# Cross attention with layer norm on one core: two buffers for the doubled queries, a compact K spread by DMA, V placed by halves

## What is computed

```python
qs = (q @ wq).reshape(Bq, Lq, H, HD).transpose(0, 2, 1, 3)
ks_ = (k @ wk).reshape(Bq, Lk, H, HD).transpose(0, 2, 1, 3)
vs = (v @ wv).reshape(Bq, Lk, H, HD).transpose(0, 2, 1, 3)
scores = jnp.einsum('bhqd,bhkd->bhqk', qs, ks_) / jnp.sqrt(jnp.float32(HD))
scores = jnp.where(mask[:, None, :, :], -jnp.inf, scores)
attn_w = jax.nn.softmax(scores, axis=-1)
attn = jnp.einsum('bhqk,bhkd->bhqd', attn_w, vs)
attn = attn.transpose(0, 2, 1, 3).reshape(Bq, Lq, H * HD)
out = attn @ wo + q
mu = jnp.mean(out, axis=-1, keepdims=True)
var = jnp.mean((out - mu) ** 2, axis=-1, keepdims=True)
return (out - mu) / jnp.sqrt(var + EPS) * gamma + beta
```

## Time and profile before

| | us |
|---|---|
| median of 3 runs | 651.32 |
| lowest and highest | 650.71, 651.92 |
| the profiled execution, its own time | 653.43 |
| its span, first to last instruction | 651.6 |
| granted clock, mean over the span | 0.987 |
| PE busy in the span | 612.8 (94%) |
| DVE, ACT, POOL busy | 526.4, 507.1, 493.8 |

### The profile page before, as it was taken

One profiled execution on the slowest core, in us unless ns is written; L12 is line 12 of the kernel. 1 busy time (PEld: TensorE's weight loads), 2 busy tenths in 40 slices (PEclk: granted clock), 3 DMA queues, 4 the chain that ended last, 5 costly groups with the idle time before them and its releaser, 6 DMA issues.

```text
span 651.6 us, 12679 instructions
## 1 busy us (share of the span) xinstructions
PE 612.8 (94%) x3840; PEld 477.7 (73%) x3840; DVE 526.4 (81%) x1008; ACT 507.1 (78%) x1558; POOL 493.8 (76%) x639
## 2 busy tenths in 40 slices
PE   7999879989999999999999999999999999999895
PEld 5676667777868777787867777786877778687763
DVE  5887667778879888888879787887888888787887
ACT  4877867878878788887978888797977888786750
POOL 5476548787968879797986879698886979576784
PEclk9999998999999999999999999999999999998998
DMA  8853455282743628273552728255361826534103
GB/s 284 211 138 104 120 146 146 74 219 81 189 146 106 169 73 220 82 203 122 137 161 95 198 69 222 101 156 156 104 185 64 226 83 163 194 100 128 49 33 114
DMA packets 47794, 90.80 MB, mean 139 GB/s; under 512 B 10096, under 2 KB 13168, under 8 KB 47728
## 3 DMA queue, kind: packets, MB, share of 16 engines
q1 hardware_dynamic: 47728, 90.00, 48.5%
HBM read 39.53 MB, written 16.78 MB: 86 GB/s over the span
## 4 chain that ended last, share of the span: by engine, by line
PE 47%; DVE 15%; DMA 13%; ACT 9%; SPq 8%; issue 4%; POOL 4%; POOLq 0%; DVEq 0%; ACTq 0%
PE bank L486 14%; PE bank L391 13%; DMA qd<-qn 12%; ACT pr L604 6%; SPq L295 4%; PE bank L428 4%; PE bank L459 4%; PE bank L438 3%; DVE pr L745 3%; PE bank L413 3%; DVE nm L751 3%; DVE sm L758 2%; SPq L267 2%; PE bank L464 2%; DVE al L767 2%
## 5 line engine op out<-in xcount | busy, mean ns | idle before, releaser
L604 ACT ACTIVATE pr<-pr,nm 128x77 f32<-128x77 f32 x1024 | 269.8, 348 | 61.8 <-DVE nm L751 59.4
L916 POOL TENSOR_TENSOR pn<-pr,rec 128x512 f32<-128x512 f32 x128 | 134.8, 1053 | 102.1 <-DVE rec L760 97.0
L745 DVE SCALAR_TENSOR_TENSOR pr<-msk,bank 128x308 f32<-128x308 uint8 x256 | 109.4, 468 | 55.9 <-PE bank L428 50.4
L391 PE MATMUL bank<-xh,wqh 128*128 128x512 f32 x256 | 104.9, 410 | 3.1 <-DVE ql L733 2.3
L758 DVE TENSOR_REDUCE sm<-pr 128x8 f32<-128x616 f32 x128 | 99.8, 779 | 9.8 <-ACT pr L604 8.6
L486 PE MATMUL bank<-woh,ah 128*128 128x512 f32 x256 | 105.5, 412 | 1.5 <-DVE al L767 1.4
L751 DVE TENSOR_REDUCE nm<-pr 128x8 f32<-128x616 f32 x128 | 101.8, 795 | 4.4
L566 ACT ACTIVATE ptr<-bank 128x512 f32<-128x512 f32 (+1 forms) x256 | 95.5, 427 | 11.8 <-PE bank L438 11.6
L486 PE MATMUL bank<-wol,ah 128*128 128x512 f32 x256 | 102.6, 401 | 0.0
L486 PE MATMUL bank<-woh,al 128*128 128x512 f32 x256 | 102.4, 400 | 0.0
L391 PE MATMUL bank<-xh,wql 128*128 128x512 f32 x256 | 100.7, 393 | 0.0
(11 more groups left out here) (81 smaller groups left out, 999.0 us busy)
## 6 DMA issues: line engine op xcount, KB each, us to landing
qd<-qn SPq DMA_DIRECT2D x120, 256.0 KB, 4.6
xraw<-xT SPq DMA_DIRECT2D x58, 256.0 KB, 3.1
xres<-x SPq DMA_DIRECT2D x58, 256.0 KB, 2.8
out<-y SPq DMA_DIRECT2D x56, 256.0 KB, 2.1
ptr<-xT SPq DMA_DIRECT2D x6, 256.0 KB, 9.4
zt<-x SPq DMA_DIRECT2D x6, 256.0 KB, 4.3
out<-zt SPq DMA_DIRECT2D x6, 256.0 KB, 2.0
wk_sb<-wk SPq DMA_DIRECT2D x4, 256.0 KB, 4.4
```

The costliest lines, as they stand in the source:

```text
L391: last = nc.tensor.matmul(misc_bank(("q", i))[:], w[:, k, m * P:(m + 1) * P], s[:, blk % 2, k, :], start=(k == 0 and n == 0), stop=(k == K ...
L604: last = nc.scalar.activation(s, s, ACT.Exp, bias=nm[:, t % 2, h:h + 1], scale=1.0)
L745: nc.vector.scalar_tensor_tensor(out=pr[:, 4 * g:4 * g + 4, :], in0=msk[:, b % 2, t % TB, :].unsqueeze(1).broadcast_to([P, 4, LK]), scalar ...
L916: nc.gpsimd.tensor_tensor(pn[:, half, 0:4, :].rearrange("p s (e k) -> p (s e) k", e=2), pr[:, hs, 0:KM], rec[:, t % 2, hs].unsqueeze(2).br ...
```

## The change

**Doubled q.** `qd` gets a second buffer: block blk uses `qd[:, blk % 2]`. `double_q(i)` now copies one part (four DMAs of 64 rows by 512 values, half of the bytes each), with a semaphore `d_qd[m]` per part, as soon as ACT has kept that part; it waits for the scores of the block two before. The calls stand in tiles t % 4 = 1, 2, 3 (for part i = t + 3) and a second one in t % 4 = 3 (i = t + 4).

**K.** `keep_k` and `low_k` are one instruction each per group of heads (128 rows) and write compact tensors `khc` and `klc`. `spread` copies them with four DMAs of 32 rows on the diagonals of `kh`, which now holds one batch; `place_kh(b, i)` does this for groups 2i and 2i + 1 when the last tile of the batch before has read them (tiles 15, 31, 47). `kd` holds two batches and is filled by `place_kd(b)`, eight DMAs, in tiles 1, 12, 20 and 36. Before tile 0 PE waits for the spread high part (`d_kh[0]`) and low part (`d_kl`, kept in the second buffer of `kd`, which is called `kl`).

**Scores.** Block 0 has three matmuls of 308 columns per group; from tile 4 on all tiles use `qd` and `kd`. In each block's first tile PE waits for one part's copies at each group. `project_q(3)` now stands ahead of the first scores, not behind.

**V.** `place_v(b, e)` does half of the rows of a batch. Batch 0's halves are in tile 0, the other six in tiles 3 to 8, one in each; PE and ACT wait per batch (`d_vb`).

```diff
-DOUBLES = {2: 4, 4: 6}
+KD_AT = {1: 0, 12: 1, TB + 4: 2, 2 * TB + 4: 3}
-PLACE = {0: (0, 0), 2: (1, 1), 4: (2, 1), 5: (3, 2)}
+PLACE = {3: (1, 0), 4: (1, 1), 5: (2, 0), 6: (2, 1), 7: (3, 0), 8: (3, 1)}
...
-        kh = sb("kh", [P, NG, NB, GW], f32r)
-        kd = sb("kd", [P, NG, 2, NB, PW], f32r)
+        khc = sb("khc", [P, NG, NB, LK], f32r)
+        klc = sb("klc", [P, NG, NB, LK], f32r)
+        kh = sb("kh", [P, NG, GW], f32r)
+        kd = sb("kd", [P, 2, NG, 2, PW], f32r)
...
-        qd = sb("qd", [P, 2, NG, D], f32r)
+        qd = sb("qd", [P, 2, 2, NG, D], f32r)
...
+            def spread(dst, src, sig):
+
+                for j in range(4):
+                    rows = slice(32 * j, 32 * j + 32)
+                    sp.dma_start(dst[rows, :, j * LK:(j + 1) * LK].bitcast(f32), src[rows].bitcast(f32)).then_inc(sig, 16)
+
+            def place_kh(b, i):
+
+                sp.wait_ge(p_s, NG * (TB * b - 1) + 2 * i + 2)
+                spread(kh[:, 2 * i:2 * i + 2], khc[:, 2 * i:2 * i + 2, b], d_kh[i])
+
+            def place_kd(b):
+
+                if b >= 1:
+                    sp.wait_ge(p_s, NG * max(4, TB * (b - 1)))
+                for v, src in enumerate((khc, klc)):
+                    for j in range(4):
...
             def double_q(i):
 
                 blk, m = i // 4, i % 4
-                if blk > 1:
-                    sp.wait_ge(p_s, NG * (4 * blk - 1) + m + 2)
-                elif m > 0:
-                    sp.wait_ge(p_s, NG * (PLAIN + 1))
-                sp.wait_ge(a_qh, i + 2)
+                if blk >= 2:
+                    sp.wait_ge(p_s, NG * 4 * (blk - 1))
+                sp.wait_ge(a_qh, i + 1)
                 for u in range(2):
                     for v in range(2):
-                        sp.dma_start(qd[64 * v:64 * v + 64, u, m:m + 2].bitcast(f32), qn[64 * u:64 * u + 64, m:m + 2].bitcast(f32)
-                                     ).then_inc(d_qd[m // 2], 16)
+                        sp.dma_start(qd[64 * v:64 * v + 64, blk % 2, u, m].bitcast(f32), qn[64 * u:64 * u + 64, m].bitcast(f32)
+                                     ).then_inc(d_qd[m], 16)
...
-                if t % 4 == 3 and 3 < t < T - 4:
-                    double_q(t + 1)
+                if t in KD_AT:
+                    place_kd(KD_AT[t])
+                if 1 <= t <= T - 4 and t % 4 > 0:
                     double_q(t + 3)
+                if t % TB == TB - 1 and t < T - 1:
+                    place_kh(t // TB + 1, 0)
+                    place_kh(t // TB + 1, 1)
+                if t % 4 == 3 and t < T - 4:
+                    double_q(t + 4)
...
-                    if r == 0 or t == PLAIN + 1:
-                        pe.wait_ge(d_qd[g // 2], 64 * blk)
...
+                    if r == 0:
+                        pe.wait_ge(d_qd[g], 64 * blk)
+                    if t == 4 or t > 4 and t % TB == 0:
+                        pe.wait_ge(d_kd[t // TB % 2], 128 * (t // TB // 2 + 1))
...
             def keep_k(g):
                 act.wait_ge(p_k, g + 1)
-                for j in range(4):
-                    rows = slice(32 * j, 32 * j + 32)
-                    nc.scalar.activation(kh[rows, g, :, j * LK:(j + 1) * LK],
-                                         bank[g][rows, 0:NB * LK].rearrange("p (b k) -> p b k", b=NB), ACT.Copy,
-                                         scale=SCALE).then_inc(a_k, 1)
+                nc.scalar.activation(khc[:, g].rearrange("p b k -> p (b k)"), bank[g][:, 0:NB * LK], ACT.Copy,
+                                     scale=SCALE).then_inc(a_k, 1)
```

More of the change, by code:

```diff
@@ L166, in cross_attention_layernorm @@
         d_wv = sem("d_wv")
-        d_vm = [sem(f"d_vm{i}") for i in range(2)]
+        d_vb = [sem(f"d_vb{b}") for b in range(NB)]
         d_msk, d_gb = [sem(f"d_msk{i}") for i in range(2)], sem("d_gb")
@@ L172, in cross_attention_layernorm @@
         d_y = [sem(f"d_y{i}") for i in range(YS)]
-        d_kd = [sem(f"d_kd{g}") for g in range(NG)]
-        d_k0 = [sem(f"d_k0{i}") for i in range(2)]
-        d_qd = [sem(f"d_qd{i}") for i in range(2)]
+        d_kh = [sem(f"d_kh{i}") for i in range(2)]
+        d_kl, d_kd = sem("d_kl"), [sem(f"d_kd{i}") for i in range(2)]
+        d_qd = [sem(f"d_qd{g}") for g in range(NG)]
         d_end, d_xe = sem("d_end"), sem("d_xe")
@@ L280, in pair_k0 @@
-            def pair_k0(g):
-                sp.wait_ge(p_s, NG * PLAIN + g + 2)
-                sp.dma_start(kd[0:64, g:g + 2, 1, 0].bitcast(f32), kh[64:128, g:g + 2, 0, PW:GW].bitcast(f32)).then_inc(d_k0[g // 2], 16)
+                        for s in range(4):
+                            row = KM * e + KR * s + KR
+                            sp.dma_start(vr[row + KM - LK:row, b, :, s % 2, :],
+                                         vs[at + KM - lo:at + LK - lo, i, s, e]).then_inc(d_vb[b], 16)
@@ new lines, in spread @@
+            def spread(dst, src, sig):
[10 more added lines that the diff above has]
+                    for j in range(4):
+                        rows = slice(64 * v + 32 * (j % 2), 64 * v + 32 * (j % 2) + 32)
+                        sp.dma_start(kd[rows, b % 2, :, j // 2, j % 2 * LK:(j % 2 + 1) * LK].bitcast(f32),
+                                     src[32 * j:32 * j + 32, :, b].bitcast(f32)).then_inc(d_kd[b % 2], 16)
@@ L306, in _ @@
             sp.wait_ge(g_z, 1)
+            sp.wait_ge(a_k, NG)
+            spread(kh, khc[:, :, 0], d_kh[0])
+            sp.wait_ge(v_k, NG)
+            spread(kl, klc[:, :, 0], d_kl)
             for n in range(8, 10):
                 load_slice(n)
-            for g in range(NG):
-                pair_k(g)
             for k in range(2):
@@ L330, in _ @@
                     sp.wait_ge(g_vz, 1)
+                    sp.wait_ge(a_v, 1)
+                    place_v(0, 0)
+                    place_v(0, 1)
                 if t in PLACE:
-                    b, piece = PLACE[t]
-                    sp.wait_ge(a_v, piece + 1)
-                    place_v(b)
+                    b, e = PLACE[t]
+                    sp.wait_ge(a_v, (1, 2, 2, 3)[b])
+                    place_v(b, e)
                 if t in (TB + 1, 2 * TB + 1):
@@ L641, in _ @@
                 keep_x(k)
-            act.wait_ge(v_z, 1)
-            keep_k(0)
-            keep_k(1)
+            for g in range(NG):
+                keep_k(g)
             keep_q(0)
             keep_q(1)
-            keep_k(2)
             keep_x(4)
             keep_q(2)
-            keep_k(3)
             keep_x(5)
@@ L653, in _ @@
             keep_x(6)
+            keep_x(7)
             exps(0, 0)
-            keep_x(7)
             keep_v(0)
@@ L712, in low_k @@
             def low_k(g):
-                for j in range(4):
-                    rows = slice(32 * j, 32 * j + 32)
-                    dve.wait_ge(a_k, 4 * g + j + 1)
-                    nc.vector.scalar_tensor_tensor(
-                        out=(kd[rows, g, 1] if j >= 2 else kt[rows, g])[:, :, j % 2 * LK:(j % 2 + 1) * LK],
-                        in0=bank[g][rows, 0:NB * LK].rearrange("p (b k) -> p b k", b=NB), scalar=SCALE,
-                        in1=kh[rows, g, :, j * LK:(j + 1) * LK].bitcast(f32), op0=ALU.mult,
-                        op1=ALU.subtract).then_inc(v_k, 1)
+                dve.wait_ge(a_k, g + 1)
+                nc.vector.scalar_tensor_tensor(
+                    out=klc[:, g].rearrange("p b k -> p (b k)"), in0=bank[g][:, 0:NB * LK], scalar=SCALE,
+                    in1=khc[:, g].rearrange("p b k -> p (b k)").bitcast(f32), op0=ALU.mult, op1=ALU.subtract).then_inc(v_k, 1)
             def mask_all(b):
```

96 lines of the change are left out of this document (32 added, 64 removed).

## The result

| | before | changed |
|---|---|---|
| median of 4 runs, us | 651.37 | 629.62 |
| lowest and highest, us | 650.71, 651.92 | 629.06, 631.12 |
| profiled execution, us | 653.43 | 630.17 |
| its span, us | 651.6 | 628.4 |
| granted clock, mean | 0.987 | 0.998 |

The ratio is 0.967, with a 95% interval of 0.965 to 0.969. The forecast was 627.5 us, in a range of 621 to 642.

What follows compares the result with a forecast made beforehand. PE's own instruction list was taken as the bound. Gains and losses 18.3 - 2.0 + 6.4 + 1.5 - 1.2 + 0.8 = 23.8 us took the profiled 653.43 to 629.6, so 627.5 us for the median, range 621 to 642.

Steps and rivals of the forecast that it cites:

- rival D: Mid-kernel: another engine takes over once PE no longer pauses, half the stalls return as waits for ACT; 636 us, chance 0.07.
- Block turns, 18.3 us: Turns between blocks: PE's weight-load waits for copies into `qd` go with halved copies and a second buffer; gain 18.3 us.
- The landing, 3.7 us: Block turns: part 3's last copy lands 3.7 us after issue, taken between 2.7 and 4.6, so no stall.
- Rival B: Block turns: part 3's last copy still lands 5.6 us or more after issue, halving gains nothing; 642 us, chance 0.12.
- Batch turns, minus 2.0 us: Tiles 16, 32, 48: `kh`'s eight DMAs delay part 3's copies, 0.7 us late each; loss 2.0 us (1 to 10).
- V and x, 6.4 and 1.5 us: Tiles 1 to 8: x slices go out earlier; PE's gap and slow clock go (6.4), part of ACT's 3.00 wait (1.5).
- Tile 4, minus 1.2 us: Tile 4 now needs doubled q, part 3 kept only one tile earlier; PE waits 0 to 2.7 us, 1.2 taken.
- The first scores: Start: K's spread copies land at 25.1 us, PE comes at 25.7, no stall; at the other end 6.2 us lost.
- rival C: Start: low K lands behind x, costing 6.2 us and a slow clock of 2 to 3; 635 to 637 us, chance 0.12.
- Costed at nothing: Mid-kernel: `kd`'s DMAs in tiles 12, 20, 36 and SP's eight more issues per block, covered by SP's 266.0 us wait for POOL.
- Rival E: Whole kernel: SP becomes the bound, slower from 1.97 us an issue; 682 us at 2.1 us an issue, chance 0.04.
- Rival F: Block turns: stalls only move from `qd` to `kh` and the ring without a gain; 651 us, chance 0.03.

Runs made afterwards that it cites:

- joined copies: Changed kernel with two buffers kept, but two parts of q in one copy (256 KB) as in the kernel before: 659.79 us, ratio 1.011.
- three kernels with idle DMAs: Changed kernel with eight, three or six small unread copies issued ahead of part 3's copies at ten ordinary turns: 671.05, 628.24 and 647.45 us.
- part 3 ahead: Changed kernel with part 3's copies of q issued ahead of the second half of `kh` at the three batch turns: 628.54 us, ratio 0.965.
- `kd` early: Changed kernel with the eight DMAs filling `kd` for batch 0 issued in tile 0 instead of tile 1: 629.59 us, ratio 0.966.
- both: Changed kernel with part 3's copies ahead of the second half of `kh` and batch 0's `kd` one tile earlier: 627.01 us, ratio 0.962.
- second profile of the kernel: The changed kernel run again without any edit, as base on the chip of three variants: 630.83 us, ratio 0.967.
- V's halves alone: Kernel before with only the V part of the change, V placed by halves in tiles 0 and 3 to 8: 644.72 us, ratio 0.990.
- V whole: Changed kernel with V placed a whole batch at a time again, batches 1 to 3 in tiles 2, 4, 5: 640.63 us, ratio 0.981.

## Why the prediction was right, point by point

- **The bound.** Right: PE's idle time came back nearly whole, and no other engine took its place (rival D). The new waits of PE for ACT or DVE in mid-kernel did not come; one for DVE of 1.27 us came at 578.5, near the end.
- **Block turns, 18.3 us.** The weight loads' 18.3 was the better of the two numbers: by the time over each turn, the thirteen turns from tile 12 on had lost 1.1 to 2.4 us each beyond today's 12.2, 19.2 us in all. At the ordinary ones nothing is left.
- **The landing, 3.7 us.** Mis-sized, on the safe side: 2.2 to 2.4 at an ordinary turn, below the low bound of 2.7. I had taken a value between two sizes at different fillings of the queue; the joined copies show that the fall from 5.97 to 2.4 comes from the halving itself. The slack is 2.4 us where 1.3 were predicted. Rival B needed 5.6. The prediction's other estimate, four fixed times of 2 us one behind the other and so 8 us from the first issue to the last landing, did not come true either: it is 4.2 us, so the four overlap.
- **Batch turns, minus 2.0 us.** The mechanism and its place were right, the size was not: by the time over the turn 2.3, 0.4 and 0.8 us are left at tiles 16, 32 and 48, 3.4 in all, within the bounds of 1 to 10. What was missing is the packet of the instruction queue at tile 16, where the last copy took 3.90 us to land, against 2.43 at tile 32. In the three kernels with idle DMAs it comes only 1.9 to 2.0 us behind the last issue there, the copy lands in 2.4, and 0.6 to 0.7 us are left at tile 16; with that, the three turns would keep 1.7 to 1.8, close to the 2.0.
- **V and x, 6.4 and 1.5 us.** Right in place and nearly in size. By the ends of the same groups PE won 1.25 us between tile 5's second and third group, where the 1.5 stood, and 6.2 between the end of tile 7 and tile 8's third group, where the 6.4 stood. Slice 12 was issued at 53.28 us where 53 was worked out. Slice 15 was issued at 82.42 and not at about 78, so that ACT still waits 1.67 us for it. The number of issues ahead of it was counted right and SP hardly waits there (0.2 us from 53 to 83), but they took 51 us instead of 46.4: the 20 copies of q took 15.3 instead of 13, with single issues of 1.0 to 1.9 us among them, the loads 0.6 more, and the short gaps between issues, 1.3 in all, had been left out.
- **Tile 4, minus 1.2 us.** The number came true, a wait of 0.86 us at the matmul and 1.1 at the weight load, but by luck. The copies were taken to land 5 to 8 us behind the keeping. That they did (5.8 us) goes with the packet of the instruction queue in their flight. In the five profiles without one (part 3 ahead, `kd` early, both, three and eight idle DMAs) the last copy lands 4.1 to 4.6 us behind the first issue, and PE comes at most 0.1 us too early for it.
- **Tile 8.** No step foresaw that it waits for its copies too, 0.84 us at the matmul and 1.1 by the ends of the groups. It comes with such a packet again, and not in the second profile of the kernel, where none is in flight. This wait is most of why the start gave 6.1 us and not the 7.5 to which its four terms sum.
- **The first scores.** Right, and rival C was not: the eight spread copies of K landed in 2.0 to 3.6 us, the last at 23.6, and PE came at 25.7, the very time predicted, without a wait:

```profile
16.93 2.71 SPq L271 DMA_DIRECT2D kh<-khc  x4
19.68 2.54 SPq L271 DMA_DIRECT2D kd<-klc  x4
```

```profile
25.68 0.31 PE L425 MATMUL bank<-kh,ah 128*128 128x308 f32 x1
```

- **The end.** The half clock at 638.7 us went too, 1.6 us. It stood in the range but not in the sum. The one at 594.4 stood in neither, and went without a gain. The range's lower end, 621, is explained as the sum without its minus terms and with the 3.00 whole; these give 622.8, and only with this clock's 1.7 it is 621.
- **Costed at nothing.** SP's `kd` and additional issues cost nothing in mid-kernel: 132.4 us of waiting for POOL are left. Rival E needed 1.97 us an issue; it is 0.60. Rival F is out.

In the sum: the start gave 6.1 us instead of 7.5, the block turns 15.2 instead of 16.3 (18.3 less 2.0), and the end 2.0 that the sum did not have. The misses cancel in part, so that 630.17 for the profiled execution against 629.6 is closer than the terms deserve.

What stays open: whether moving the packet of the instruction queue alone would move the landings with it, and why half clock comes behind the same stall in one execution and not in another.

## What to carry to other kernels

When an engine waits for a chain of copies, look at which copy is issued last, how many bytes are queued with it and when it is wanted; part it so that little goes out last. Ask of each queue what else has to go out in that same stretch: a second buffer paid less by freeing its own tensor than by taking eight issues out of the tile in which another one's copies were due. A wait that is cured by reordering goes to the copy that is now last, so count the issues between the last producer and the first consumer before reordering. When one copy of a kind lands late and its twins do not, look at the other DMA queues in its flight, and don't credit an edit with a wait that is also missing in a second profile of the unedited kernel.

## What the runs showed of the hardware

- Four queued SBUF-to-SBUF copies of 64 rows land 2.2 to 2.4 us after their issue at 128 KB each (at the ordinary turns; 3.0 to 3.7 for the four of tile 4, with the small copies of V around them), and 3.0, 3.9, 4.5 and 5.97 at 256 KB, growing from copy to copy. The first three of four issues cost SP some 0.5 to 0.6 us each at both sizes, the fourth 0.7 on average at 128 KB and 1.3 at 256. The idle DMAs of 0.65 us land in 1.8.
- The queue that the profile calls "instruction" moves 16 KB packets of 0.9 to 2.0 us on the same DMA engines. In 11 of 11 cases in which the last copy of 128 KB took over 3.2 us to land, one had started between 0.2 us before and 2.0 us after its issue; without one the same copy took at most 3.0, mostly 2.4.
- A PE stall of 2.6 to 3.2 us was followed by half clock for 3.41 us in 4 of 4 cases with joined copies and 7 of 10 with eight idle DMAs, where 2.80 us went without it and 2.61 with it. Behind stalls of 1.0 to 1.5 at the block turns there was mostly none, but at the turn to tile 60 there was one behind 1.11 us in the kernel before and behind 1.13 in the one with V's halves alone, each with 0.37 us more of idle time shortly after. Stalls between these go either way: at tile 16 2.05 us without in the changed kernel's first profile and 2.37 without with V whole; 2.19, 2.04 and 1.69 with it in others, and at tile 52 1.77 with it. Near 60 us it also came behind a stall of only 1.21, in the second profile of the changed kernel and not in the first. A stretch of 3.41 us cost 1.6 us by the ends of the same matmuls, so that a stall of 2.7 us that has one behind it costs some 4.3 in all.
